# Counting edge pairs: turnings and the logarithm of a pair placed among the next pair's chunks

## The chip, the cores and the metric

The kernel runs on one core of one Trainium2 chip. The metric is the device time of one execution in microseconds (us). Before the change three runs gave 9569.98, 9573.84 and 9581.71 us, so the median is 9573.84 us.

## The reference, cut to what matters

Four graph layers follow each other on 3125 nodes. Three of them read the same edges (103125 with the self loops). The change touches only a preparation whose two results the second and the third layer use.

```python
# layer 1, attention over all edges into a node
e = leaky_relu(alpha_s[src] + alpha_d[dst])
alpha = exp(e - emax[dst]) / (segment_sum(exp(e - emax[dst]), dst)[dst] + eps)
out = segment_sum(xs[src] * alpha, dst)
# layer 2, convolution
agg = segment_sum(h[src], dst)
```

An edge enters either sum as often as it occurs. So both can be written over a dense matrix C, where C[i, j] is the number of edges from j to i: the convolution multiplies by C, the attention adds ln C to its logits. The kernel computes C and ln(C + 2^-60), in which it presses the entries of zero counts far down, and stores both to HBM in f32 as `c.counts` and `c.logs`.

## The kernel before, in words

`count_pairs` (L1078) does this, once, after the edges have been grouped and before the layers. The nodes are ranked into NB = 25 blocks of 128. Two blocks form a pair, so there are PAIRS = 13 of them (the last has one block). The lists of a pair's nodes come in groups of 64 neighbour slots; `steps` (L1136) loads from the tile `groups` how many groups a pair has (`many`) and which is its first (`first`). Every engine runs its own program over the pairs, with semaphores between them.

For each group:

- SP (L1143) loads the ids when DVE has released the one buffer (`ids_free`).
- DVE (L1323) splits an id into high and low part (to L1345), PE transposes the two parts (`split_ps`, L1202), DVE casts them (L1350) and makes `hi_hot` (L1352), a one-hot of the block.
- Then come CHUNKS_OF = 8 chunks of 16 nodes. For each, DVE makes `lo_hot` (`hot`, L1356), PE multiplies the two one-hots in 32 small matmuls (L1212), and ACT copies the sums from PSUM to `counts` (L1243; in a group after a pair's first one DVE adds instead, L1370). `lo_hot` and `chunk_ps` have two buffers each: `hot` of chunk u waits for chunk u - 2 (`counted`), and the matmuls of chunk u wait for the copy of chunk u - 2 (`kept`).

When the chunks of a pair are done, four things follow:

- The turning: PE transposes each block of counts (L1193) in quads of 4 transpositions into one of two PSUM tiles, ACT copies each quad out (L1254). TURNS = 7 quads for each of the two blocks make 14 quads, of 50 transpositions. A quad waits for the copy of the quad two before (`moved`).
- The store of the turned counts, 3.2 MB, issued by ACT (L1258).
- The logarithm, one ACTIVATE by ACT over 6400 elements per partition (L1262).
- `tell`: DVE presses down the zero entries (L1378), then ACT issues the store of the logarithms, 3.2 MB (L1267).

The order is written out by hand in the loops at the end of each engine's program. Quoted from PE and ACT:

```python
with pe.Fori(0, PAIRS // 2 - 1) as two:
    for k in range(2):
        pair(two * 2 + (k + 1))
        turn_counts(two * 2 + k, k, 2)
with act.Fori(0, PAIRS // 2 - 1) as two:
    for k in range(2):
        pair(two * 2 + (k + 2), k)
        finish(two * 2 + (k + 1), 1 - k, two + k)
        tell(two * 2 + k, k)
```

So PE turns pair p after all chunks of pair p + 1, and ACT copies the turned counts and takes the logarithm of pair p there too. DVE runs `pair(p + 2)`, then `tell(p)`. `counts`, `logs` and `turned_sb` have two buffers each.

## Time and profile before

| | before |
|---|---|
| median of 3 runs | 9573.84 us |
| the profiled execution | 9577.8 us |
| its span | 9575.8 us |
| mean granted clock of TensorE | 0.803 of full |
| the stage of `count_pairs` in the span | 1493 to 1899 us |

The profiled execution is 4 us above the median, and 2 us of it lie outside its span. The stage of `count_pairs` is about 4% of the span. The engines in it repeat one pattern from pair to pair, so that it is read from the timeline of one pair, and the stages before and after it are the same program in both kernels.

### The profile page before, as it was taken

What the parts mean: (1) busy time and instruction counts of PE and PEld (TensorE: products, weight loads), DVE (VectorE), ACT (ScalarE), POOL (GpSimd) and SP (SyncE); (2) the same over time, 40 slices, a digit from 0 to 9 for tenths busy, and PEclk for the clock granted to TensorE, in tenths of its full rate; (3) what the DMA queues carried; (4) which work ended last, traced back from release to release, by engine and by line L of the source; (5) the groups of instructions that cost most, each with busy time, mean ns of one, the idle gap of its engine ahead of it and who ended that gap; (6) DMA issues with size and microseconds to landing.
All of it is one profiled execution on the core that took longest, in us unless ns stands there. A gap on an engine that the chain in (4) does not pass through costs nothing. (4 is left out here: it accounts for less than half of the span.)

```text
span 9575.8 us, 217005 instructions
## 1 busy us (share of the span) xinstructions
PE 6368.2 (67%) x63738; PEld 5150.9 (54%) x63739; DVE 7308.4 (76%) x20527; ACT 5592.6 (58%) x12073; POOL 6322.6 (66%) x5522
## 2 busy tenths in 40 slices
PE   3894796555555565546655478878878869467775
PEld 2893796444444444434444355555555544366665
DVE  9779777667777577766777799989989970388886
ACT  4224325546665566656666489979979950144443
POOL 0777773067776777767777578858858850377776
PEclk8555555678887788877788799999999989788887
DMA  0210114622222222222222222212212237232322
GB/s 12 65 53 2 59 61 139 232 48 52 53 52 42 52 52 52 52 43 51 52 52 52 48 56 56 56 50 56 57 42 62 56 93 280 76 53 54 54 54 50
DMA packets 411419, 617.79 MB, mean 65 GB/s; under 512 B 267559, under 2 KB 324353, under 8 KB 387609
## 3 DMA queue, kind: packets, MB, share of 16 engines
q0 software_dynamic: 185232, 370.99, 16.7%
q1 hardware_dynamic: 158592, 160.26, 5.4%
q10 hardware_dynamic: 67497, 85.32, 2.5%
q8 instruction: 50, 0.82, 0.0%
q14 instruction: 48, 0.39, 0.0%
HBM read 513.10 MB, written 104.66 MB: 65 GB/s over the span
## 5 line engine op out<-in xcount | busy, mean ns | idle before, releaser
L914 POOL DMA_INDIRECT l_land<-table,l_words x3504 | 3377.2, 964 | 1115.1 <-issue 1066.6
L1871 POOL DMA_INDIRECT ell<-gat_stage_pay,gat_stage_at x816 | 1657.0, 2031 | 261.8 <-issue 248.4
L1506 PE MATMUL left_product_ps<-k_w,messageT 128*128 128x128 f32 x5136 | 882.4, 324 | 670.8 <-ACT messageT L1541 670.8
L1506 PEld LDWEIGHTS left_product_ps<-k_w,messageT 128*128 128x128 f32 x5136 | 740.9, 222 | 850.3 <-ACT messageT L1541 850.3
L1966 ACT COPY gat_probT<-gat_ps 128x512 f32<-128x512 f32 (+1 forms) x2100 | 1017.2, 552 | 71.6 <-PE gat_ps L1911 62.8
L245 POOL DMA_INDIRECT ell<-pay,position x816 | 843.1, 1033 | 289.3 <-issue 280.0
L1557 ACT ACTIVATE weighed<-kept,l_prob 128x128 f32 x3120 | 988.2, 390 | 68.6 <-ACT l_prob L1059 68.6
L1059 ACT ACTIVATE l_prob<-l_shifted,l_fall 128x9 f32<-128x9 f32 x506 | 153.3, 303 | 1493.5 <-DVE l_fall L1053 1485.5
L2429 PE MATMUL rel_ps<-relation_parts,hot 128*128 128x128 bf16 x11328 | 789.2, 241 | 338.7 <-DVE hot L2530 338.3
L2429 PEld LDWEIGHTS rel_ps<-relation_parts,hot 128*128 128x128 bf16 x11328 | 766.5, 110 | 361.6 <-DVE hot L2530 361.5
L296 PE MATMUL looked_ps<-count,loT_wide 128*128 (+1 forms) x3264 | 755.6, 384 | 47.5 <-issue 44.3
L296 PEld LDWEIGHTS looked_ps<-count,loT_wide 128*128 128x128 f32 x3264 | 744.6, 333 | 56.4 <-issue 53.8
L1911 PE MATMUL gat_ps<-ident,gat_logit 128*128 128x128 f32 x3750 | 579.0, 286 | 254.0 <-ACT gat_logit L1958 242.9
L1669 DVE TENSOR_REDUCE part<-weighed 128x128 f32<-128x1024 f32 x390 | 742.9, 1905 | 0.0
L1917 PE MATMUL gat_ps<-gat_probT,h 128*32 128x128 f32 x15000 | 703.1, 281 | 0.3
L1046 DVE CUSTOM_DVE_ANT_0 product<-right,left_now 128x128 f32<-128x128 f32 x3120 | 697.7, 287 | 0.1
L1911 PE MATMUL gat_ps<-ident,work 128*128 128x128 f32 x3750 | 573.8, 284 | 178.2 <-ACT work L1958 162.5
L354 ACT CAST loT_wide<-loT 128x512 f32<-128x512 bf16 x408 | 252.3, 619 | 700.4 <-PE looked_ps L300 672.4
L1492 PE MATMUL rel_ps<-relation_parts,hotT 128*128 128x256 bf16 x3888 | 659.7, 317 | 2.0 <-ACT hotT L1536 2.0
L1911 PEld LDWEIGHTS gat_ps<-ident,gat_logit 128*128 128x128 f32 x3750 | 408.2, 142 | 419.6 <-ACT gat_logit L1958 275.3
L1500 PE MATMUL left_turned_ps<-ident,message 128*128 128x128 f32 x2568 | 489.8, 323 | 170.3 <-DVE message L1661 170.0
L1911 PEld LDWEIGHTS gat_ps<-ident,work 128*128 128x128 f32 x3750 | 402.8, 140 | 343.2 <-ACT work L1958 247.4
(351 smaller groups left out, 14927.2 us busy)
## 6 DMA issues: line engine op xcount, KB each, us to landing
gcn_edges<-counts SPq DMA_DIRECT2D x50, 1600.0 KB, 8.0
l_land<-table,l_words POOLq DMA_INDIRECT x3504
rows<-low_dram SPq DMA_DIRECT2D x34, 1536.0 KB
counts<-pair_turned_sb ACTq DMA_DIRECT2D x12, 3200.0 KB
logs<-pair_logs ACTq DMA_DIRECT2D x12, 3200.0 KB, 18.2
ell<-pay,position POOLq DMA_INDIRECT x816
ell<-gat_stage_pay,gat_stage_at POOLq DMA_INDIRECT x816
l_words<-ell SPq DMA_DIRECT2D x446, 8.0 KB
```

Of the source, the lines that this page charges most:

```text
L245: pool.indirect_dma_start(c.ells[0][:, :], bass.IndirectOffsetOnAxis(ap=position[:, 0, t:t + 1], axis=0), pay[:, t, :], None).then_inc(pla ...
L296: pe.matmul(looked_ps[r % HALVES][:, j, :], loT_wide[:, r % CAST, j, :], count[:, bass.ds(tile + j, 1), :].rearrange("p a n -> p (a n)"), ...
L914: pool.indirect_dma_start(self.land[:, p, s, :], None, table[:, :], bass.IndirectOffsetOnAxis(ap=self.words[:, p, s, 0:1], axis=0)).then_i ...
L1046: return self.nc.vector.tensor_tensor_reduce(product, rows, own, op0=ALU.mult, op1=ALU.add, scale=-1.0, scalar=0.0, accum_out=self.fall[:, ...
L1506: mm = pe.matmul(right_ps[:, k * H + j, :], messageT[:, k, j, :], k_w[:, :], start=True, stop=True)
L1557: last = nc.scalar.activation(weighed[:, s, :], kept[:, bass.ds(n % 2, 1), s, :].rearrange("p a d -> p (a d)"), ACT.Copy, scale=soft.prob[ ...
L1669: V.tensor_reduce(part[:, :], weighed[:, :, :].rearrange("p s f -> p f s"), AX.X, ALU.add)
L1871: pool.indirect_dma_start(c.ells[1][:, :], bass.IndirectOffsetOnAxis(ap=stage_at[n % 2][:, t:t + 1], axis=0), stage_pay[n % 2][:, t, :], N ...
L1911: mm = pe.transpose(ps[:, q % 4, r * P:(r + 1) * P], logit[t % 2][:, j * P:(j + 1) * P], c.ident[:, :])
L1917: mm = pe.matmul(ps[C * r:C * (r + 1), 4 + t % 2, 0:P], xs[:, 4 * q + r, t * C:(t + 1) * C], probT[:, q % 4 * 4 + r, :], start=(q == 0), s ...
L1966: nc.scalar.copy(probT[:, q % 4 * 4:q % 4 * 4 + rows_of(q), :].rearrange("p r d -> p (r d)"), ps[:, q % 4, 0:rows_of(q) * P]).then_inc(mov ...
L2429: mm = pe.matmul(rel_ps[:, k * H + s, :], hot[:, k, g, s, :], parts[:, g, t, :], start=(g == 0 and t == 0), stop=(g == PARTS - 1 and t == 2))
```

## The change

- `groups` is one word for each pair, `many` in its low and `first` in its high half. `steps` loads one word where it loaded two, on each of four engines, and PE calls it once for each pair instead of twice. DVE packs the word in two more instructions, once.
- PE: `turn_quad` does one quad. In `pair(p)`, after chunks 1, 3, 5 and 7, an `If` for the first group encloses 3, 4, 3 and 4 quads of pair p - 1. Only the 7 quads of the last pair stand alone.
- ACT: in `pair(p)`, the copies of those quads follow the copies of the same chunks. The logarithm of pair p - 1 is in four pieces, after the copies of chunks 2, 4, 6 and 7 (1536, 1536, 1536 and 1792 elements per partition). Before the first piece ACT waits for the store of the logarithms that the buffer held. After the loop it issues the store of the counts.
- DVE: `tell(p - 2)` is in two pieces inside `pair(p)`, before `hot` of chunk 2 and of chunk 5. It counts `told` after the last `hot`, with a drain ahead.
- SP: loads the ids of three pairs, then in turn those of pair p + 3 and, having waited for `told`, stores the logarithms of pair p.

```diff
-        groups = sb("pair_groups", [P, 2, PAIRS], I32)
+        groups, firsts = sb("pair_groups", [P, PAIRS], I32), sb("pair_firsts", [P, PAIRS], I32)
...
+        TELL_AT = {2: slice(0, NB // 2), 5: slice(NB // 2, NB)}
+
+        def quads_of(u):
+            return range(2 * TURNS * (u // 2) // (CHUNKS_OF // 2), 2 * TURNS * (u // 2 + 1) // (CHUNKS_OF // 2)) if u % 2 else ()
+
+        LOG_AT = {u: slice(NB * n // 4, NB * (n + 1) // 4) for n, u in enumerate((2, 4, 6, 7))}
...
-            many = eng.value_load(groups[0:1, 0, bass.ds(p, 1)], min_val=1, max_val=z.bodies)
-            first = eng.value_load(groups[0:1, 1, bass.ds(p, 1)], min_val=0, max_val=z.bodies)
-            return many, first
+            word = eng.value_load(groups[0:1, bass.ds(p, 1)], min_val=1, max_val=(1 << 31) - 1)
+            many = (word & ((1 << HALF_BITS) - 1)).with_bounds(min_val=1, max_val=z.bodies)
+            return eng.snap(many), eng.snap((word >> HALF_BITS).with_bounds(min_val=0, max_val=z.bodies))
...
+                def tell(p, k, parts=2):
+                    sp.wait_ge(told, p + 1)
+                    sp.dma_start(c.logs.rearrange("(h p) j -> p h j", p=P)[:, :, bass.ds(p * (2 * P), parts * P)],
+                                 logs[k][:, :, 0:parts, :]).then_inc(logs_out[k], 16)
+
+                for p in range(3):
+                    pair(p)
+                with sp.Fori(0, PAIRS // 2 - 1) as two:
+                    for k in range(2):
+                        pair(two * 2 + (k + 3))
+                        tell(two * 2 + k, k)
+                tell(PAIRS - 3, 0)
+                tell(PAIRS - 2, 1)
+                tell(PAIRS - 1, 0, 1)
...
-                def turn_counts(p, k, parts):
...
+                def turn_quad(p, k, q):
+                    b, t = q // TURNS, q % TURNS
+                    pe.wait_ge(moved, p * (2 * TURNS) + (q + 1))
+                    for r in range(4 * t, min(4 * t + 4, NB)):
+                        mm = pe.transpose(turned_ps[q % 2][:, r - 4 * t, :], counts[k][:, r, b, :], c.ident[:, :])
+                    mm.then_inc(turned, 1)
+
+                def chunk(n, u):
+                    pe.wait_ge(hot_ready, n * CHUNKS_OF + (u + 1))
+
+                    pe.wait_ge(kept, n * CHUNKS_OF + (u + 1))
...
+                    mm.then_inc(counted, 1)
+
+                def pair(p, k, earlier=True):
                     many, first = steps(pe, p)
                     with pe.Fori(0, many) as g:
                         n = pe.snap(first + g)
...
                         for u in range(CHUNKS_OF):
+                            chunk(n, u)
+                            if earlier and quads_of(u):
+                                with pe.If(g < 1):
+                                    for q in quads_of(u):
+                                        turn_quad(p + (-1), 1 - k, q)
+
+                pair(0, 0, earlier=False)
+                with pe.Fori(0, PAIRS // 2) as two:
                     for k in range(2):
+                        pair(two * 2 + (k + 1), 1 - k)
+                many, first = steps(pe, PAIRS - 1)
+                pe.wait_ge(kept, (first + many) * CHUNKS_OF + 2)
+                for q in range(TURNS):
+                    turn_quad(PAIRS - 1, 0, q)
...
+                def turn_out(p, k, q):
+                    b, t = q // TURNS, q % TURNS
+                    rows = min(4, NB - 4 * t)
+                    act.wait_ge(turned, p * (2 * TURNS) + (q + 1))
+                    nc.scalar.copy(turned_sb[k][:, b, 4 * t * P:(4 * t + rows) * P],
+                                   turned_ps[q % 2][:, 0:rows, :].rearrange("p r d -> p (r d)")).then_inc(moved, 1)
+
+                def send(p, k, parts=2):
+                    act.wait_ge(moved, p * (2 * TURNS) + (parts * TURNS + 2))
+                    act.dma_start(c.counts[bass.ds(p * (2 * P), parts * P), :].rearrange("(b p) i -> p b i", p=P),
+                                  turned_sb[k][:, 0:parts, :]).then_inc(counts_out[k], 16)
+
+                def log(k, rows, parts=2):
+                    return nc.scalar.activation(logs[k][:, rows, 0:parts, :], counts[k][:, rows, 0:parts, :], ACT.Ln,
+                                                bias=few[:, 0:1])
+
+                def pair(p, k, sent=None, again=True):
                     many, first = steps(act, p)
-                    if not unused:
+                    if again and sent is not None:
                         act.wait_ge(logged, p + (-1))
+                    if sent is not None:
+                        act.wait_ge(counts_out[1 - k], sent * 16 + 16)
                     with act.Fori(0, many) as g:
                         n = act.snap(first + g)
                         with act.If(g < 1):
...
+                                if sent is not None:
+                                    for q in quads_of(u):
+                                        turn_out(p + (-1), 1 - k, q)
+                                    if u == min(LOG_AT):
+                                        act.wait_ge(logs_out[1 - k], sent * 16 + 16)
+                                    if u in LOG_AT:
+                                        last = log(1 - k, LOG_AT[u])
+                            if sent is not None:
+                                last.then_inc(logged, 1)
+                    if sent is not None:
+                        send(p + (-1), 1 - k)
+
+                pair(0, 0)
+                pair(1, 1, 0, again=False)
                 with act.Fori(0, PAIRS // 2 - 1) as two:
                     for k in range(2):
+                        pair(two * 2 + (k + 2), k, two + k)
+                pair(PAIRS - 1, 0, PAIRS // 2 - 1)
+                act.wait_ge(counts_out[0], PAIRS // 2 * 16 + 16)
+                for q in range(TURNS):
+                    turn_out(PAIRS - 1, 0, q)
+                send(PAIRS - 1, 0, 1)
...
-                V.tensor_copy(groups[:, 0, :], groups_f[:, :])
-                v.drain()
-                V.tensor_tensor(groups[:, 1, :], ends_f[:, :], groups_f[:, :], ALU.subtract)
+                v.drain()
+                V.tensor_tensor(firsts[:, :], ends_f[:, :], groups_f[:, :], ALU.subtract)
+                v.drain()
+                V.tensor_scalar(firsts[:, :], firsts[:, :], HALF_BITS, None, ALU.logical_shift_left)
+                v.drain()
+                V.tensor_tensor(groups[:, :], firsts[:, :], plan_j[:, :], ALU.bitwise_or)
...
+                def tell(p, k, rows):
+                    v.wait_ge(logged, p + 1)
+                    flat = logs[k][:, rows, :, :].rearrange("p h b j -> p (h b j)")
+                    return V.scalar_tensor_tensor(out=flat, in0=flat, scalar=-NEG, in1=flat, op0=ALU.mult, op1=ALU.min)
+
+                def pair(p, k, earlier=False):
...
                             for u in range(2, CHUNKS_OF):
+                                if earlier and u in TELL_AT:
+                                    tell(p + (-2), k, TELL_AT[u])
                                 v.wait_ge(counted, n * CHUNKS_OF + (u - 1))
                                 hot(u)
+                            if earlier:
+                                v.drain()
+                                v.sem_inc(told, 1)
...
                 pair(0, 0)
                 pair(1, 1)
                 with v.Fori(0, PAIRS // 2 - 1) as two:
                     for k in range(2):
+                        pair(two * 2 + (k + 2), k, True)
+                pair(PAIRS - 1, 0, True)
+                for p in range(PAIRS - 2, PAIRS):
+                    tell(p, p % 2, slice(0, NB)).then_inc(told, 1)
```

On ACT, in the loop over pairs, the compiled program of before has behind the last quads (`pair_turned_sb` is the turned copy, `pair_turned_ps` its PSUM tile):

```order
L1253 REGISTER_ALU
L1254 COPY pair_turned_sb<-pair_turned_ps 128x128
L1257 REGISTER_ALU
L1258 ISA
L1258 DMA counts<-pair_turned_sb 128x2x3200
L1262 ACTIVATE pair_logs<-pair_counts,pair_few 128x6400
L1267 ISA
L1267 DMA logs<-pair_logs 128x25x256
```

The changed one has at the start of a pair and up to the fourth chunk:

```order
L1275 COMPARE_AND_BRANCH
L1277 ISA
L1278 ACT_TABLE_LOAD
L1278 COPY pair_counts<-pair_chunk_ps 128x2x25x16
...
L1255 COPY pair_turned_sb<-pair_turned_ps 128x512
L1277 REGISTER_ALU
L1278 COPY pair_counts<-pair_chunk_ps 128x2x25x16
L1264 ACT_TABLE_LOAD
L1264 ACTIVATE pair_logs<-pair_counts,pair_few 128x1536
L1277 REGISTER_ALU
L1278 COPY pair_counts<-pair_chunk_ps 128x2x25x16
```

The logarithm has moved between the copies of two chunks, and the loop now holds two table loads for each pair; before, the only one of this stage stands ahead of the loop.

On PE, between the last chunk and the first quad, before:

```order
L1212 MATMUL pair_chunk_ps<-pair_hi_hot,pair_lo_hot 128x25 x32
L1198 REGISTER_ALU
L1198 COMPARE_AND_BRANCH
L1137 ISA
L1137 TENSOR_LOAD pair_groups
L1137 ISA x2
L1138 ISA
L1138 TENSOR_LOAD pair_groups
L1138 ISA x2
L1187 ISA
L1191 ISA
L1193 MATMUL pair_turned_ps<-ident,pair_counts 128x128 x4
```

Now, behind the second chunk:

```order
L1215 MATMUL pair_chunk_ps<-pair_hi_hot,pair_lo_hot 128x25 x32
L1231 COMPARE_AND_BRANCH
L1203 ISA
L1205 MATMUL pair_turned_ps<-ident,pair_counts 128x128 x4
L1203 REGISTER_ALU
L1205 MATMUL pair_turned_ps<-ident,pair_counts 128x128 x4
L1203 REGISTER_ALU
L1205 MATMUL pair_turned_ps<-ident,pair_counts 128x128 x4
L1231 UNCONDITIONAL_BRANCH
L1209 REGISTER_ALU
L1215 MATMUL pair_chunk_ps<-pair_hi_hot,pair_lo_hot 128x25 x32
```

The two loads ahead of the quads are gone; a branch stands there, and the next chunks wait behind the quads in PE's order.

## Rows read from the trace of the kernel before

**Rows 1.** The page: span, section 1.

```profile
span 9575.8 us, 217005 instructions
```

**Rows 2.** Waits, stage of `count_pairs`: engine, line, releaser, total us, times, longest.

```profile
DVE pair_splitT L1350 <- PE pair_split_ps L1202: 80.9, 13, 11.5
ACT pair_counts L1243 <- PE pair_chunk_ps L1212: 78.4, 94, 27.1
...
PE pair_chunk_ps L1212 <- DVE pair_lo_hot L1356: 54.9, 51, 3.6
...
ACT pair_logs L1262 <- DMA logs<-pair_logs: 7.7, 1, 7.7
```

**Rows 3.** Timeline of PE: start, us, line and operation, idle before.

```profile
1504.08 0.69 PE L1202 MATMUL pair_split_ps<-ident,pair_split 128*128 128x128 f32 x2 [18.35 <-DVEq L1346]
...
1520.45 0.69 PE L1202 MATMUL pair_split_ps<-ident,pair_split 128*128 128x128 f32 x2 [2.12 <-DVEq L1346]
...
1576.33 0.68 PE L1202 MATMUL pair_split_ps<-ident,pair_split 128*128 128x128 f32 x2 [1.77 <-issue]
1580.57 2.34 PE L1212 MATMUL pair_chunk_ps<-pair_hi_hot,pair_lo_hot 64*128 64x25 bf16 x64 [3.55 <-DVE pair_lo_hot L1356]
...
1588.19 2.36 PE L1212 MATMUL pair_chunk_ps<-pair_hi_hot,pair_lo_hot 64*128 64x25 bf16 x64 [0.18 <-DVE pair_lo_hot L1356]
1592.98 5.24 PE L1193 MATMUL pair_turned_ps<-ident,pair_counts 128*128 128x128 f32 x25 [2.43 <-issue]
1598.69 1.09 PE L1193 MATMUL pair_turned_ps<-ident,pair_counts 128*128 128x128 f32 x8 [0.46 <-ACT pair_turned_sb L1254]
...
1604.41 0.43 PE L1202 MATMUL pair_split_ps<-ident,pair_split 128*128 128x128 f32 x2 [1.40 <-issue]
...
1831.13 0.43 PE L1202 MATMUL pair_split_ps<-ident,pair_split 128*128 128x128 f32 x2 [1.18 <-issue]
```

**Rows 4.** Timeline of DVE: the same columns.

```profile
1589.19 6.82 DVE L1378 SCALAR_TENSOR_TENSOR pair_logs<-pair_logs 128x6400 f32<-128x6400 f32 x1
...
1604.88 0.43 DVE L1350 CAST pair_splitT<-pair_split_ps 128x256 bf16<-128x256 f32 x1 [6.39 <-PE pair_split_ps L1202]
...
1881.29 6.83 DVE L1378 SCALAR_TENSOR_TENSOR pair_logs<-pair_logs 128x6400 f32<-128x6400 f32 x1 [8.85 <-ACT pair_logs L1262]
```

**Rows 5.** Timeline of ACT and of its queue (ACTq).

```profile
1594.98 0.59 ACT L1254 COPY pair_turned_sb<-pair_turned_ps 128x512 f32<-128x512 f32 x1 [0.27 <-PE pair_turned_ps L1193]
...
1603.92 5.64 ACT L1262 ACTIVATE pair_logs<-pair_counts,pair_few 128x6400 f32<-128x6400 f32 x1 [0.61 <-ACT pair_turned_sb L1254]
...
1609.88 1.73 ACT L1243 COPY pair_counts<-pair_chunk_ps 128x800 f32<-128x800 f32 x2 [0.31 <-PE pair_chunk_ps L1212]
...
1878.30 2.96 ACT L1262 ACTIVATE pair_logs<-pair_counts,pair_few 128x3200 f32<-128x3200 f32 x1 [7.73 <-DMA logs<-pair_logs]
```

**Rows 6.** Windows: stretch, us, busy (x count) of PE, PEld, DVE, ACT, POOL, clock, DMA share, GB/s.

```profile
1576.30:1604.40 28.10, 18.91 (x308) 15.85 (x308) 20.38 (x24) 19.06 (x24) 8.21 (x7) 0.64 0.79 266
1592.90:1596.00 3.10, 3.02 (x14) 2.67 (x15) 3.10 (x3) 1.25 (x3) 0.00 (x0) 0.50 1.05 334
1596.00:1599.00 3.00, 2.40 (x16) 1.63 (x15) 2.03 (x14) 2.39 (x5) 0.00 (x0) 0.92 0.22 63
1612.00:1618.00 6.00, 5.58 (x158) 5.36 (x158) 5.59 (x6) 3.96 (x5) 0.00 (x0) 0.50 0.99 333
```

**Rows 7.** Groups by line, in the stage: busy, mean ns, idle before.

```profile
L1352 DVE TENSOR_TENSOR pair_hi_hot<-pair_hi_iota,pair_splitT 128x3200 bf16<-128x3200 bf16 x13 | 23.7, 1826 | 1.0
...
L1262 ACT ACT_TABLE_LOAD x1 | 1.3, 1283 | 0.5 <-ACT pair_turned_sb L1254 0.5
```

**Rows 8.** DMA of the stage: issues with median us to landing; SP's first issue behind it.

```profile
logs<-pair_logs ACTq DMA_DIRECT2D x12, 3200.0 KB, 18.2
...
1899.49 0.87 SPq L2717 DMA_DIRECT2D x<-table_h  x1
```

More of the change, by code:

```diff
@@ L1145, in _, with pair @@
                 sp.wait_ge(plan_ready, 1)
-                def pair(p, _):
+                def pair(p):
                     many, first = steps(sp, p)
@@ L1159, in pair @@
                                          .rearrange("(n p s) c -> p n (s c)", p=P, s=S)).then_inc(ids_in, 16)
-                each_pair(sp, pair)
+                def tell(p, k, parts=2):
[11 more added lines that the diff above has]
+                tell(PAIRS - 1, 0, 1)
+                for k in range(2):
+                    sp.wait_ge(logs_out[k], (PAIRS + 1 - k) // 2 * 16 + 16)
             @block.gpsimd
@@ L1183, in _ @@
                 pe.wait_ge(plan_ready, 1)
-                def turn_counts(p, k, parts):
-                    many, first = steps(pe, p)
-                    pe.wait_ge(kept, (first + many) * CHUNKS_OF + 2)
-                    for b in range(parts):
-                        for t in range(TURNS):
-                            q = b * TURNS + t
-                            pe.wait_ge(moved, p * (2 * TURNS) + (q + 1))
-                            for r in range(4 * t, min(4 * t + 4, NB)):
-                                mm = pe.transpose(turned_ps[q % 2][:, r - 4 * t, :], counts[k][:, r, b, :], c.ident[:, :])
-                            mm.then_inc(turned, 1)
-                def pair(p):
+                def turn_quad(p, k, q):
[7 more added lines that the diff above has]
+                    pe.wait_ge(kept, n * CHUNKS_OF + (u + 1))
+                    for j in range(CHUNK):
+                        for b in range(2):
+                            half = slice(b * GROUP, (b + 1) * GROUP)
+                            mm = pe.matmul(chunk_ps[u % 2][:, b, j * NB:(j + 1) * NB], lo_hot[half, u % 2, :, j],
+                                           hi_hot[half, :, u * CHUNK + j], start=True, stop=True)
+                    mm.then_inc(counted, 1)
+                def pair(p, k, earlier=True):
                     many, first = steps(pe, p)
@@ L1273, in _ @@
+                            if sent is not None:
[4 more added lines that the diff above has]
+                pair(1, 1, 0, again=False)
                 with act.Fori(0, PAIRS // 2 - 1) as two:
                     for k in range(2):
-                        pair(two * 2 + (k + 2), k)
-                        finish(two * 2 + (k + 1), 1 - k, two + k)
-                        tell(two * 2 + k, k)
@@ L1278, in _ @@
-                pair(PAIRS - 1, 0)
-                finish(PAIRS - 2, 1, PAIRS // 2 - 1)
-                tell(PAIRS - 3, 0)
-                finish(PAIRS - 1, 0, PAIRS // 2, 1)
-                tell(PAIRS - 2, 1)
-                tell(PAIRS - 1, 0, 1)
+                        pair(two * 2 + (k + 2), k, two + k)
[3 more added lines that the diff above has]
+                    turn_out(PAIRS - 1, 0, q)
@@ L1373, in pair @@
                                     hot(u + 2)
-                def tell(p, k):
-                    v.wait_ge(logged, p + 1)
-                    flat = logs[k][:, :, :, :].rearrange("p h b j -> p (h b j)")
-                    V.scalar_tensor_tensor(out=flat, in0=flat, scalar=-NEG, in1=flat, op0=ALU.mult,
-                                           op1=ALU.min).then_inc(told, 1)
                 pair(0, 0)
@@ L1384, in _ @@
                     for k in range(2):
-                        pair(two * 2 + (k + 2), k)
-                        tell(two * 2 + k, k)
-                pair(PAIRS - 1, 0)
-                for p in range(PAIRS - 3, PAIRS):
-                    tell(p, p % 2)
+                        pair(two * 2 + (k + 2), k, True)
+                pair(PAIRS - 1, 0, True)
+                for p in range(PAIRS - 2, PAIRS):
+                    tell(p, p % 2, slice(0, NB)).then_inc(told, 1)
 def attention_over_relations(nc, top, z, c, a, x, h, res, work):
```

50 lines of the change are left out of this document (2 added, 48 removed).

## The prediction

> **What bounds the kernel now.** I read the page first: the span is 9575.8 us [rows 1]; the profiled execution took 9577.8 us, 4 us above the median of 9573.84. The stage changed lies between 1493 and 1899 us, so everything here is decided in some 400 us. The waits of that stage come next [rows 2]. Nobody waits for one engine alone: DVE waits 80.9 us for PE's split transpositions, ACT 78.4 us for chunks, PE 54.9 us for DVE's one-hots. So no engine is the bound; a chain that goes from engine to engine is. The timeline of PE shows it for one pair [rows 3]. From the split transpositions at 1576.33 to the first chunk at 1580.57 pass 4.24 us, in which DVE casts and makes hi_hot (1.83 us [rows 7]) and the first lo_hot. The eight chunks run to 1590.55, two in 2.34 to 2.36 us. Then PE idles 2.43 us: end of a loop, two loads of registers, the copy of chunk 7. The 50 transpositions take 1592.98 to about 1603.0, and after 1.40 us more the next split transpositions start, at 1604.41. Sum: 28.1 us a pair. In this cycle DVE is busy 20.4 us and ACT 19.1 us [rows 6].
>
> What hides what: DVE's `tell` of 6.82 us lies beside PE's turning, and DVE still idles 6.39 us behind it before the cast [rows 4]. ACT's logarithm of 5.64 us starts at 1603.92 [rows 5] and lies beside the 4.24 us in which PE and DVE prepare the next pair; chunk copies start 0.31 us behind it. Both are off the chain now.
>
> **The change part by part.** The pieces of `tell` move from hidden to hidden: I cost them at nothing. The first (3072 of 6400 elements, 3.3 us) stands before the third lo_hot, beside the first three quads (2.7 us); the other (3.5 us) lies beside PE's wait below. What they would cost without this cover is up to 6.8 us a pair.
>
> The logarithm is the piece that matters. It leaves the preparation, where ACT has nothing else to do, and goes between copies that PE waits for. From 5.64 us for 6400 elements and 2.96 us for 3200 [rows 5], an ACTIVATE costs 0.28 us plus 0.84 us per 1000 elements; so three pieces of 1536 cost 1.57 us each, the one of 1792 1.78 us. Four pieces are 6.5 us instead of 5.64. The order of the changed program also has a table load before the first copy and before the first piece of every pair. One took 1.28 us [rows 7]. The former lies in ACT's idle preparation and costs nothing while ACT is ahead there by about 1 us; the latter stands between the copies of chunks 2 and 3. The Trainium skill, "ScalarE activation tables: per-element evaluation and per-set limits", section "What a function is on this engine", says that two functions in one set need no switch; the copies between the logarithms of before ran without a load, so the trace agrees. By that rule the loads would be absent and the forecast below would fall by some 12 us; the program's order has them all the same, and I count them.
>
> Now I walk through one pair, time 0 being its split transpositions, with PE at half clock. Chunks: 1.18 us each. Quads: 14 transpositions took 3.02 us at granted clock 0.50 [rows 6], with a hand-over about 0.9 us a quad. Copy of a chunk 0.83 us (two in 1.73 [rows 5]), of a quad 0.59 us plus 0.08.
>
> - Chunks 0 and 1 end at 6.6, quads 0 to 2 at 9.3, chunk 2 at 10.6, chunk 3 at 11.8, quads 3 and 4 at 13.6.
> - ACT: copy of chunk 2 to 11.4, table load to 12.7, piece of the logarithm to 14.3, copy of chunk 3 to 15.1, quad 3 to 15.8. Quad 5 needs the PSUM tile of quad 3, so **PE waits 2.2 us**.
> - Quads 5 and 6 to 16.9, chunks 4 and 5 to 19.4, quads 7 and 8 to 21.2. ACT has copied quad 7 only at 22.1 (a piece lies between chunks 4 and 5): wait 0.9.
> - Quad 9 to 23.0, chunks 6 and 7 to 25.4, quads 10 and 11 to 27.2; quad 10 is copied at 28.1: wait 0.9. Quads 12 and 13 to 29.3.
> - One load of a register instead of two before the next split: 1.40 to 1.77 us in [rows 3]; I take 0.9. That is 30.2. Some ten hand-overs of 0.07 to 0.1 us and the branches of the four `If`s bring it to **31.0 us**.
>
> Against 28.1 us: gone are the 2.43 us before the turning and 0.5 us of loads; back come 4.0 us of waits for ACT, 1.3 us for quads that all run at half clock, and hand-overs. For the `If`s the trace has no row on PE. Bounds: nothing, when PE's sequencer runs ahead, and 2.43 us for a place that holds a branch, two loads and a wait. I take near nothing, since work is queued ahead of each.
>
> Sum over the stage. Pair 0 is as before: 1504.08 to 1520.45 [rows 3]. The eleven cycles to the last pair took 1831.13 - 1520.45 = 310.7 us, and will take 11 x 31.0 = 341.0: **+30.3 us**. The tail: before, from 1831.13 to the end of the last `tell` (1881.29 + 6.83 [rows 4]) 57.0 us and to the next stage's load at 1899.49 [rows 8] 68.4 us, for two pairs' turnings and logarithms stood there, and ACT waited 7.73 us for a store [rows 5]. After: the logarithm of pair 11 ends at 32.5, a table load and 7 quads to 39.6, table load and 2.96 us to 43.9, `tell` to 50.7; the last store of 1.6 MB is a quarter of what takes 18.2 us [rows 8] (counts and logarithms together), 4.6 us, plus 2 for issue and latency: 57.3. **-11.1 us**. Net +19.2 us: 9597.0 for the profiled execution, 9593 for the median.
>
> Packing the word on DVE adds two small operations once, under 1 us. The stores of logarithms now come from SP: issued at about 21 in one cycle, the buffer is needed at 12.7 of the next, 22.7 us later, against 18.2 us [rows 8] with both stores in flight. So no wait. Ids are loaded a pair ahead, with more room.
>
> **The rivals.**
>
> 1. *The clock rises inside the loop.* At 1592.9 the granted clock is 0.50, after 3.1 us of transpositions it is 0.92 [rows 6]; chunks alone leave it at 0.50 [rows 6]. At full clock 8 transpositions take 1.09 us [rows 3], so ACT's copy sets the pace. The waits for ACT stay, and the cycle comes to 30.0 us: 12 us less in all, 9581. Against it: at most four quads stand together, and chunks and waits come between. The Trainium skill, "TensorE: Matmul & The Clock Gate", section "What's actually happening", says that activity releases the throttle, which by itself would bear out this case. Chance 0.22.
> 2. *Faster: PE's waits for ACT vanish.* Place: quads 5, 9 and 12. If ACT's detour between copying chunk 2 and copying quad 3 (4.4 us) were shorter than the 2.2 us that PE needs for chunk 3's end and quads 3 and 4, the cycle would be 27.0 less hand-overs, 26.6 us. That is 11 x (26.6 - 28.24) = -18 us, and the tail is 4.4 shorter: 33.5 us off, 9540. It decides from a cycle of about 27.8 us down. For it: absent table loads together with rival 1; against it: the durations of [rows 5, 7]. Chance 0.13.
> 3. *Branches cost.* At 0.5 us for each `If`, 2 us a pair and 24 us in all: 9617. For it: 1.40 us of [rows 3] are nothing but such work. Against it: the queued matmuls. Chance 0.12.
> 4. *Stores collide.* If logarithms need over 22.7 us to land, ACT waits before the first piece; 2 us a pair give the same 9617. Chance 0.04.
>
> That the change does nothing is excluded: the 13 makings of hi_hot [rows 7] mean one group a pair, so every `If` is taken.
>
> **How the numbers follow.** A measurement of this kernel can tell about 0.2%, 19.1 us. The forecast has 0.49 and stands at that bound; errors of 0.5 us a cycle put it at 9587 to 9599, half on either side, a little more above, for what I left at nothing can only add. Slower: 0.30 of it, and rivals 3 and 4, 0.46. Within 0.2%: 0.19, and 0.22 of rival 1, 0.41. Faster: 0.13. The range goes from 9562, between rivals 1 and 2, to 9614, most of rival 3.
>
> **What would show it.** In the profile after: split transpositions 31 us apart; PE idle before quads 5, 9 and 12 released by the turned copy; 24 table loads or so in the stage; granted clock near 0.5; DVE's `tell` in two forms with no one waiting for it; last `tell` some 50 us behind the last split. Wrong, if the cycle is under 28.1 us, or if the idle time of PE is released by DVE or called issue.

## The result and the profile after

Over seven runs of each, on one chip, the median went from 9577.62 us (9569.98 to 9581.73) to 9613.95 us (9597.9 to 9617.91): ratio 1.0034, 95% interval 1.0025 to 1.0044. So the change makes this kernel slower by 0.34%, 36.3 us. The prediction had 9593.0 us, in a range from 9562.0 to 9614.0, whose upper end the median meets to within 0.05 us, and gave "slower by over 0.2%" 0.46.

The execution that was profiled was the fastest of the seven, 9597.9 us against 9577.8 us before: 20.1 us more, where the forecast had 19.2. The page gives its span, beside which [rows 1] stand:

```profile
span 9596.1 us, 216930 instructions
```

I cut the traces at the first operations of the stages. The stage of `count_pairs` takes 433.0 us instead of 414.9, the three behind it 3542.5, 2378.4 and 435.9 instead of 3540.3, 2376.9 and 437.2, and the rest is the same within 0.2 us. So 18.1 of the 20.3 us of span are where the diff is. The other 16 us between this execution and the median are in no trace. The profiled execution has a mean granted clock of 0.798, the six others have 0.793 to 0.795; whether that goes with the 16 us is not shown.

One pair of the changed kernel, from its split transpositions to the next; the timeline of PE, with the columns of [rows 3]:

```profile
1580.60 0.68 PE L1225 MATMUL pair_split_ps<-ident,pair_split 128*128 128x128 f32 x2 [1.58 <-issue]
1584.83 2.35 PE L1215 MATMUL pair_chunk_ps<-pair_hi_hot,pair_lo_hot 64*128 64x25 bf16 x64 [3.55 <-DVE pair_lo_hot L1384]
1587.11 2.90 PE L1205 MATMUL pair_turned_ps<-ident,pair_counts 128*128 128x128 f32 x12
1590.37 2.35 PE L1215 MATMUL pair_chunk_ps<-pair_hi_hot,pair_lo_hot 64*128 64x25 bf16 x64 [0.36 <-DVE pair_lo_hot L1384]
1592.65 1.97 PE L1205 MATMUL pair_turned_ps<-ident,pair_counts 128*128 128x128 f32 x8
1596.60 1.33 PE L1205 MATMUL pair_turned_ps<-ident,pair_counts 128*128 128x128 f32 x5 [1.98 <-ACT pair_turned_sb L1255]
1597.86 2.22 PE L1215 MATMUL pair_chunk_ps<-pair_hi_hot,pair_lo_hot 64*128 64x25 bf16 x64
1600.01 1.97 PE L1205 MATMUL pair_turned_ps<-ident,pair_counts 128*128 128x128 f32 x8
1602.66 1.12 PE L1205 MATMUL pair_turned_ps<-ident,pair_counts 128*128 128x128 f32 x4 [0.68 <-ACT pair_turned_sb L1255]
1603.71 2.28 PE L1215 MATMUL pair_chunk_ps<-pair_hi_hot,pair_lo_hot 64*128 64x25 bf16 x64
1605.92 1.97 PE L1205 MATMUL pair_turned_ps<-ident,pair_counts 128*128 128x128 f32 x8
1608.54 1.33 PE L1205 MATMUL pair_turned_ps<-ident,pair_counts 128*128 128x128 f32 x5 [0.65 <-ACT pair_turned_sb L1255]
1611.12 0.68 PE L1225 MATMUL pair_split_ps<-ident,pair_split 128*128 128x128 f32 x2 [1.26 <-issue]
```

Chunks and quads alternate as the diff says. PE stops three times for ACT: before quad 5 (1.98 us here, 2.33 to 2.44 in six of ten pairs), before quad 9 (0.68) and before quad 12 (0.65). From the third split, at 1549.75, to the last, at 1856.66, ten cycles take 30.69 us each; before it was 28.33 us. PE also waits 0.36 us for the lo_hot of chunk 2, which DVE makes behind the first piece of `tell`.

Where the first of these stops comes from is to be seen on ACT (the same columns):

```profile
1591.62 0.83 ACT L1278 COPY pair_counts<-pair_chunk_ps 128x800 f32<-128x800 f32 x1 [0.98 <-PE pair_chunk_ps L1215]
1592.47 1.28 ACT L1264 ACT_TABLE_LOAD   x1
1593.77 1.58 ACT L1264 ACTIVATE pair_logs<-pair_counts,pair_few 128x1536 f32<-128x1536 f32 x1
1595.25 0.81 ACT L1278 COPY pair_counts<-pair_chunk_ps 128x800 f32<-128x800 f32 x1
1595.95 1.08 ACT L1255 COPY pair_turned_sb<-pair_turned_ps 128x512 f32<-128x512 f32 x2
```

Between chunk 2's copy and that of quad 3 ACT loads a table and takes a quarter of the logarithm. PE has sent quads 3 and 4 by 1594.6 and stands still until quad 3 is copied.

The waits of the stage, to be read against [rows 2] (engine, line, releaser: total us, times, longest):

```profile
ACT pair_counts L1278 <- PE pair_chunk_ps L1215: 92.8, 68, 27.5
DVE pair_splitT L1378 <- PE pair_split_ps L1225: 67.8, 13, 6.9
PE pair_chunk_ps L1215 <- DVE pair_lo_hot L1384: 51.2, 27, 3.6
PE pair_turned_ps L1205 <- ACT pair_turned_sb L1255: 45.8, 39, 2.6
PE pair_split_ps L1225 <- issue: 14.8, 11, 1.6
```

The fourth row, PE's waits for ACT at the quads, was 17.4 us in the kernel before; the 28 us more are about what the loop has lost. No row of an engine's waits in this stage names a store. The window of the pair above (columns as in [rows 6]), and two rows of the groups of ACT (busy us, mean ns, idle before):

```profile
1580.60:1611.10 30.50, 22.05 (x308) 18.57 (x308) 20.47 (x25) 21.55 (x29) 4.15 (x4) 0.50 0.73 252
```

```profile
L1264 ACT ACT_TABLE_LOAD x13 | 16.7, 1283 | 0.6 <-ACT pair_turned_sb L1255 0.4
L1278 ACT ACT_TABLE_LOAD x12 | 15.4, 1283 | 8.1 <-ACT pair_logs L1264 7.7 <-issue 0.3
```

The granted clock is 0.50, the lower level of 1.2 GHz, over this whole pair; in a pair of the kernel before it was 0.64 [rows 6]. But this is not so in every pair. Another pair, a stretch in it, and the ten cycles together:

```profile
1733.90:1764.90 31.00, 21.61 (x309) 18.23 (x309) 20.50 (x25) 22.40 (x29) 0.00 (x0) 0.56 0.63 221
1744.00:1747.00 3.00, 3.00 (x69) 2.95 (x66) 2.81 (x3) 2.00 (x2) 0.00 (x0) 0.92 0.00 0
1549.75:1856.66 306.91, 217.52 (x3081) 183.63 (x3081) 204.97 (x250) 219.41 (x281) 24.46 (x19) 0.53 0.64 224
```

In six of the ten pairs the clock rises to its upper level for some 3.5 us, here after PE had worked from 1738.18 to 1743.30 (chunks 0 and 1, quads 0 to 2), and the mean of the pair is 0.56. These are the pairs in which PE waits 2.33 to 2.44 us before quad 5. In both kinds of pair chunk 2 starts 9.8 us and quad 5 16.0 us behind the split transpositions: DVE's lo_hot and then ACT set these times, and what PE gains by the clock it spends waiting.

ACT's 21.55 us of work in the first pair holds two table loads; with one more behind the loop, before the copies of the last pair's quads (1888.48), there are 26 in the stage.

The end of the stage, in the timelines of DVE and of SP's queue, to be read against [rows 4, 8]:

```profile
1899.34 6.82 DVE L1349 SCALAR_TENSOR_TENSOR pair_logs<-pair_logs 128x6400 f32<-128x6400 f32 x1 [4.31 <-ACT pair_logs L1264]
```

```profile
1917.74 0.85 SPq L2742 DMA_DIRECT2D x<-table_h  x1
```

and the last store in the list of issues (KB each, us to landing):

```profile
logs<-pair_logs SPq DMA_DIRECT2D x1, 1600.0 KB, 9.7
```

From the last split to the next stage's load pass 61.1 us; before it was 68.4. What lies behind the end of the last `tell` is as long as before: 11.6 us (from 1906.16 to 1917.74) against 11.4 (from 1888.12 to 1899.49 [rows 4, 8]). The queue that carries the stores, in the kernel before from 1888 to 1900 and in the changed one from 1906 to 1918 (packets, MB, share):

```profile
q10 hardware_dynamic: 4362, 2.80, 74.2%
q1 hardware_dynamic: 4367, 2.80, 74.4%
```

In both, 2.80 MB are moved there, some 1.2 MB more than the last store has: the rest of the stores before it is still on its way.

### The profile page after: what moved, and what is told of

The parts are those of the page before. It is cut to its first block and busy times, and to the rows that moved or that the text cites. A ratio compares the mean times of both kernels' runs of the same rounds, so it can differ in the third digit from the quotient of the medians.

```text
span 9596.1 us, 216930 instructions
## 1 busy us (share of the span) xinstructions
PE 6409.2 (67%) x63738; PEld 5190.3 (54%) x63739; DVE 7322.0 (76%) x20539; ACT 5625.0 (59%) x12134; POOL 6326.8 (66%) x5522
## 6 DMA issues: line engine op xcount, KB each, us to landing
logs<-pair_logs SPq DMA_DIRECT2D x12, 3200.0 KB, 11.2
```

## The experiments

The theory: the cycle is a chain through PE, ACT and PE; what it gained by removing PE's 2.43 us before the turning it lost by putting ACT's logarithm and a table load among the copies that PE waits for. The rivals: it is the interleaving itself, at half clock, or the branches, that cost; and, for the 16 us outside the trace, that the changed loop has a slower way of running which the profiled execution did not take.

**A word on the chips.** The runs below were made on three other chips, one group on each. On these the same kernel before takes 12875.66, 12655.4 and 12910.38 us instead of 9577.62. So whole times are given as ratios to the kernel before on the same chip, and a second measure decides: the time from the third split transpositions to the next stage's load `x<-table_h`, read from each trace. The kernel before has 351.7 us there on the first chip, 350.1 and 350.9 on two of the others; the changed one 368.0, and 367.9 and 368.5. So this stretch agrees within 1.6 us where the whole differs by over 3000.

**The changed kernel once more**, unedited.

> The changed kernel once more, for a second trace: of its seven runs one took 9597.9 us (the profiled one) and six 9609 to 9618. Theory A (the stage of the pair counting alone differs between the two kernels): split transpositions 30.5 us apart in this trace too, the stage of count_pairs 18 us longer than before, and whatever is above 9598 lies in other stages, at a lower granted clock of TensorE. Rival (the loop itself has a slower way of running): the split transpositions are 32 us apart in a trace of 9612 us, and no other stage differs.

Measured: 12856.33 us, ratio 0.999 [0.9977, 1.0003]. The cycle is 30.68 us, as on the first chip, 367.9 us by the second measure. So the loop has no slower way that shows here; that rival has nothing for it. The clock in its ten cycles is 0.51 in the mean where it was 0.53 in the first trace, with the same cycle. The ratio is another than on the first chip though the loop costs the same: something outside the loop weighs as much as the change.

**No table loads in the loop.** One logarithm of one column ahead of the loop; the compiler then puts one load into the stage instead of 26.

```diff
-        few = sb("pair_few", [P, 1])
+        few, first_ln = sb("pair_few", [P, 1]), sb("pair_first_ln", [P, 1])
...
+                nc.scalar.activation(first_ln[:, :], few[:, :], ACT.Ln, bias=few[:, 0:1])
```

> One Ln of a single column stands ahead of ACT's loop, so that the compiler places no table load inside it (the program has 1 for this stage instead of 10, 24 of them executed). Theory A (the load between the copies of chunks 2 and 3 is on the chain): PE's wait for ACT before quad 5 falls from 2.0-2.4 us to about 0.8, the cycle from 30.5 to 29.3 us, the tail loses 2.6 us: 15 to 17 us less than the changed kernel. Rival (loads lie in idle time of ACT): the cycle stays at 30.5 us and at most the 2.6 us of the tail are won.

Measured: ratio 0.9993 [0.9982, 1.0005]; cycle 29.30 us; 352.65 us, 15.3 less than the changed kernel. Quad 5 now starts 14.6 us behind the split transpositions instead of 16.0. In the pair shown PE waits 0.58 us before it; in most pairs in which the clock rises it is 1.38 to 1.45, for 2.33 to 2.44 before:

```profile
2664.90 0.68 PE L1225 MATMUL pair_split_ps<-ident,pair_split 128*128 128x128 f32 x2 [1.60 <-issue]
...
2679.50 1.33 PE L1205 MATMUL pair_turned_ps<-ident,pair_counts 128*128 128x128 f32 x5 [0.58 <-ACT pair_turned_sb L1256]
```

A table load between copies costs 1.4 us a pair, its full 1.28 us and a little more. As all of the gain lies before quad 5 and one load explains it but for 0.1 us, the one in the preparation cost next to nothing, as forecast. The tail lost 1.5 us, where 2.6 were expected.

**The logarithm whole, behind chunk 7**, without table loads and with them. It then stands beside the next pair's preparation again, as in the kernel before, while the quads stay among the chunks.

```diff
-        LOG_AT = {u: slice(NB * n // 4, NB * (n + 1) // 4) for n, u in enumerate((2, 4, 6, 7))}
+        LOG_AT = {7: slice(0, NB)}
```

> As ln_first, and the logarithm of pair p-1 is one ACTIVATE behind all copies of pair p, where it lies beside the preparation of the next pair, as before the change; the quads stay among the chunks. Theory A (what costs is the logarithm between the copies, not the quads among the chunks): PE waits for ACT before quads 5, 9 and 12 fall from 3.3 us in all to under 0.5, cycle 27.2 us or less, 33 to 40 us under the changed kernel and 0 to 10 us under the kernel before in the loop and 11 to 15 us in the tail. Rival B (interleaving itself costs: PE's strict order, quads at half clock): the cycle stays above 29 us.

Measured: ratio 0.9971 [0.9956, 0.9987]; cycle 27.41 us; 333.5 us. That is 34.5 us less than the changed kernel on the same chip and some 17 less than the kernel before on the others. The cycle is 0.2 us above what was expected, and the tail 9.0 us shorter than that of the kernel before, not 11 to 15.

```profile
2690.06 0.68 PE L1225 MATMUL pair_split_ps<-ident,pair_split 128*128 128x128 f32 x2 [1.20 <-issue]
...
2714.70 1.22 PE L1205 MATMUL pair_turned_ps<-ident,pair_counts 128*128 128x128 f32 x5 [0.38 <-ACT pair_turned_sb L1256]
...
2717.63 0.68 PE L1225 MATMUL pair_split_ps<-ident,pair_split 128*128 128x128 f32 x2 [1.70 <-issue]
```

```profile
2689.32 5.66 ACT L1265 ACTIVATE pair_logs<-pair_counts,pair_few 128x6400 f32<-128x6400 f32 x1
2695.56 0.83 ACT L1279 COPY pair_counts<-pair_chunk_ps 128x800 f32<-128x800 f32 x1 [0.58 <-PE pair_chunk_ps L1215]
```

The whole logarithm is done 0.58 us before ACT gets the first chunk of the next pair, so PE does not wait for it.

**The same with the table loads.**

> As log_last_ln_first but with the compiler's table loads in the loop: two for each pair, one before the logarithm and one before the first copy of the next pair. Theory A: both now lie in a row with the logarithm (1.28 + 5.64 + 1.28 us plus 0.9 us between), 9.1 us beside a preparation of 5.5 us up to the first copy, so that copy is 1.5 to 2.5 us late: cycle 28.5 to 29.5 us, 12 to 22 us under the changed kernel. Rival (loads cost nothing anywhere): the same cycle as log_last_ln_first.

Measured: ratio 0.9989 [0.9977, 1.0001]; cycle 28.74 us; 350.4 us. In ACT's timeline the load at L1278 now does delay the first copy:

```profile
2662.09 1.28 ACT L1264 ACT_TABLE_LOAD   x1
2663.38 5.66 ACT L1264 ACTIVATE pair_logs<-pair_counts,pair_few 128x6400 f32<-128x6400 f32 x1
2669.53 1.28 ACT L1278 ACT_TABLE_LOAD   x1 [0.49 <-ACT pair_logs L1264]
2670.82 1.55 ACT L1278 COPY pair_counts<-pair_chunk_ps 128x800 f32<-128x800 f32 x2
```

The four kernels on this chip make a square, in us a pair:

| logarithm | with table loads | without |
|---|---|---|
| four pieces among the copies | 30.68 | 29.30 |
| whole, behind chunk 7 | 28.74 | 27.41 |

The place of the logarithm costs 1.9 us in both columns, the loads 1.3 to 1.4 in both rows. With the quads among the chunks and the logarithm in its old place the cycle is 27.41 against 28.2 us before, so the rival that expected over 29 us from the interleaving falls. The 27.41 are not the interleaving alone: this kernel also has the packed word, which an experiment below finds to be worth 1.2 us a pair in the changed kernel. The interleaving by itself may then be no gain at all; it was not run by itself.

**The kernel before, the changed kernel and the best of the square together**, on another chip, with a new one beside them.

> The kernel before, unchanged, for its trace on the chip of this call. Theory A: split transpositions 28.2 us apart in the steady loop, on any chip (the changed kernel has 30.7). What the whole execution takes can differ from chip to chip (9577 us on one, 12876 us on the next for the same kernel); by theory A the added time lies outside the steady loop of the pair counting, in waits called issue. Rival: on a chip where the whole is slow the loop of before is slower too, above 29 us, which would explain why there the changed kernel was not slower than before (ratio 0.999).

Measured: ratio 1.0001 [0.9989, 1.0013]; cycle 28.17 us; 350.1 us.

> The changed kernel, unchanged, beside before_again on the same chip. Theory A: loop 30.7 us; from the third split transpositions to the next stage's load 368 us against 351.7 us of before; the first two pairs depend on the chip (46 us on the first, 77 us on the second). Rival: some other stage differs by over 5 us between the two traces of this call; then that stage, and not the loop, holds the rest of the 36 us by which the medians of the first measurement differ.

Measured: ratio 1.0086 [1.0068, 1.0104], 115 us by the medians, far more than on the first chip; cycle 30.72 us, 368.5 us: 18.4 more than the kernel before, as on the first chip. Yet the stage of `count_pairs` is longer by 28.8 us, the other 10 in its first two passes, and the attention over relations, where the diff changes nothing, by 98 us (5033.2 against 4935.1). On this chip the rival holds: another stage differs, and by far more than the loop.

> The kernel of log_last_ln_first once more (logarithm whole behind all copies, one Ln ahead of the loop), beside before_again. Loop 27.4 us, 333 to 334 us from the third split to the next load: 18 us under before and 34.5 us under the changed kernel on any chip; ratio to before 0.998 on a fast chip.

Measured: ratio 1.0076 [1.0051, 1.0101]; cycle 27.31 us; 332.8 us, and a stage 8.4 us shorter than before. Here the attention over relations takes 5028.5 us, 93 more, which hides that gain; the expected ratio was 0.998. On these chips, then, a ratio alone would mislead.

**Two quads ahead of the first chunk.** PE still idles some 3.5 us behind the split transpositions. This edit, on top of the last, turns quads 0 and 1 of the pair before in that gap, twelve others among the chunks, three at a time, and cuts `tell` in three.

```diff
-        TELL_AT = {2: slice(0, NB // 2), 5: slice(NB // 2, NB)}
+        TELL_AT = {2: slice(0, NB // 3), 4: slice(NB // 3, 2 * NB // 3), 6: slice(2 * NB // 3, NB)}
+        AHEAD = 2
...
                         mm.then_inc(split_turned, 1)
+                        if earlier:
+                            with pe.If(g < 1):
+                                pe.wait_ge(kept, n * CHUNKS_OF + 2)
+                                for q in range(AHEAD):
+                                    turn_quad(p + (-1), 1 - k, q)
...
                         with act.If(g < 1):
+                            if sent is not None:
+                                for q in range(AHEAD):
+                                    turn_out(p + (-1), 1 - k, q)
```

> As best_1, and quads 0 and 1 of the earlier pair stand between the split transpositions and chunk 0, where PE idles 3.5 us, the other 12 quads three by three; tell in three pieces. Theory A (PE's own work and the 3.5 us idle of the preparation are the chain now): two quads of 0.9 us each leave the chain and so does most of the 0.8 us wait for the lo_hot behind the second piece of tell: loop 25.0 to 25.8 us, 20 to 28 us under best_1. Rival B (ACT becomes late: 5.65 us of logarithm, then two copies of quads before the copy of chunk 0): gain under 0.8 us a pair, and PE waits for ACT before chunk 2. Rival C: DVE becomes the chain (20.5 us busy in 27): PE idles before chunks on lo_hot, loop 26 us.

Measured: 12625.13 us, ratio 0.9976 [0.9964, 0.9989]; cycle 25.20 us; 313.9 us, 36.2 less than the kernel before. One pair on PE:

```profile
2611.68 0.68 PE L1227 MATMUL pair_split_ps<-ident,pair_split 128*128 128x128 f32 x2 [2.10 <-issue]
2612.16 1.91 PE L1207 MATMUL pair_turned_ps<-ident,pair_counts 128*128 128x128 f32 x8
2615.92 2.35 PE L1217 MATMUL pair_chunk_ps<-pair_hi_hot,pair_lo_hot 64*128 64x25 bf16 x64 [1.85 <-DVE pair_lo_hot L1395]
...
2637.07 0.68 PE L1227 MATMUL pair_split_ps<-ident,pair_split 128*128 128x128 f32 x2 [1.54 <-issue]
```

and the window of this pair, with the columns of [rows 6]:

```profile
2611.68:2637.07 25.39, 21.54 (x309) 18.59 (x309) 20.36 (x26) 18.72 (x24) 0.00 (x0) 0.50 0.77 267
```

PE is busy 21.54 of 25.39 us at half clock in this pair; the pairs beside it have 0.63 and 0.57 and take 25.16 and 25.01 us. The 25.2 us are 3 us under the kernel before. How much of the 2.1 us under best_1 is due to the two quads and how much to the third piece of `tell` was not separated.

> The kernel of head_quads again, for its ratio beside before_third and the runs of before on this chip: loop 25.2 us, from the third split to the next load 314 us, 36 us under before in the stage; ratio 0.996 to 0.998 where the other stages stay as they are.

Measured, on a third chip: 12854.89 us, ratio 0.9957 [0.9941, 0.9974], a little more gain than expected; cycle 25.21 us; 314.0 us, 36.9 less than the kernel before beside it. It has the lowest median of the study on both chips where it ran, though on this one the interval overlaps with that of the kernel with two words below. On the first chip it was not run.

**Next to no work added.** The kernel before, with 40 increments of a semaphore added once at the start of the stage on each of SP, PE, ACT and DVE: 160 small instructions, which no loop repeats.

```diff
+                for _ in range(40):
+                    pe.sem_inc(turns, 1)
```

> The kernel before with 40 increments of a semaphore that nobody waits for at the start of the pair counting on SP, PE, ACT and DVE: the same work, the code behind it lies elsewhere. Theory C (where the code lies changes the waits called issue in the long loop of the attention over relations): the loop of the pair counting stays at 28.2 us a pair, the attention over relations (on two slow chips 4935 to 5100 us, depending on the kernel) differs by over 20 us from that of before_third in this call, or on a fast chip by 5 to 20 us. Rival (the changed stage itself, its data or its timing, disturbs the later stage): all stages within 5 us of before_third.

Measured: ratio 1.0141 [1.0126, 1.0155]; cycle 28.07 us.

> The kernel before, unchanged: what a second trace on a third chip differs by. Loop 28.2 us, from the third split to the next load 350 to 352 us. Beside the runs of before of the same call it says how far two identical kernels lie apart: ratio 1.000 within 0.15%.

Measured: ratio 1.0012 [0.9999, 1.0025]; cycle 28.23 us; 350.9 us. The attention over relations in the first and in the second of these two (columns as in [rows 6]):

```profile
2947.00:8185.00 5238.00, 2309.66 (x13113) 1877.14 (x13113) 2558.07 (x11073) 2254.94 (x5786) 2538.36 (x2643) 0.68 0.15 34
```

```profile
2918.40:8019.00 5100.60, 2496.29 (x13113) 2028.34 (x13113) 2567.42 (x11073) 2268.75 (x5786) 2546.40 (x2643) 0.66 0.15 35
```

The same instructions in the same numbers, no engine busy for longer, and 137 us more. The loop of `count_pairs` stays as it is; the stage as a whole takes 21 us more (467.0 against 446.3): DVE waits 43.2 us for its first ids instead of 2.7, and part of that is made up in the next two cycles. The 40 increments hold DVE itself for 3.7 us. The added increments can act on a later stage by where its code lies or by when it starts; no run separates the two, so that it is the place of the code is only argued. But on this chip an edit that adds next to no work costs 1.4%, four times what this change cost on the first.

**Two words again**, in the changed kernel.

```diff
-            word = eng.value_load(groups[0:1, bass.ds(p, 1)], min_val=1, max_val=(1 << 31) - 1)
...
+            many = eng.value_load(groups[0:1, 0, bass.ds(p, 1)], min_val=1, max_val=z.bodies)
+            first = eng.value_load(groups[0:1, 1, bass.ds(p, 1)], min_val=0, max_val=z.bodies)
...
```

> The changed kernel without the packed word (steps loads two registers as before). Theory A (the loads between the last quad and the next split transpositions lie on PE's chain): PE's idle time there rises from 1.2-1.65 us by 0.3 to 0.6, loop 31.0 to 31.3 us against 30.7, 4 to 7 us in all. Rival (the sequencer's time there is the ends of loop and branch, not the load): the same 30.7 us.

Measured: ratio 0.9968 [0.9956, 0.998]; cycle 31.93 us; 380.6 us. Two splits of its timeline, to be compared with the 1.26 and 1.58 us above:

```profile
2663.18 0.68 PE L1225 MATMUL pair_split_ps<-ident,pair_split 128*128 128x128 f32 x2 [2.80 <-issue]
...
2695.04 0.69 PE L1225 MATMUL pair_split_ps<-ident,pair_split 128*128 128x128 f32 x2 [2.55 <-issue]
```

The expectation was too low: in this kernel the second load costs 1.2 us a pair, 12 to 13 us in the stage. It is no fixed price: the kernel before has two loads in this place too, and only 1.40 and 1.77 us of idle time [rows 3]. The prediction had credited the packed word with 0.5 us a pair against the kernel before; measured from there, 1.26 and 1.58 us are 0.15 to 0.2 less. Why two loads cost so much more behind the `If` is open. (The ratio is below one though the stretch is 30 us longer than before: the attention over relations took 95 us less than in the run beside it.)

## Why the prediction was right, and where it was off

- *A chain from engine to engine is the bound, and the logarithm moved onto it.* Right, and shown: with the logarithm alone put back beside the preparation the cycle falls by 1.9 us, without the table loads by 1.4, and with both the stretch from the third split to the next load is 17 us shorter than that of the kernel before instead of 16 to 18 longer.
- *The cycle: 31.0 us.* 30.69, from about 30.5 and 30.9 in turn. The wait before quad 5 was put at 2.2 and is 1.98 to 2.44; quad 5 was put at 15.8 us behind the split and starts at 16.0. Those before quads 9 and 12 were put at 0.9 each and are 0.65 to 0.68: too large by 0.5 us together. The load before the next split was put at 0.9 and is 1.17 to 1.65, with the branches' cost in it, too small by 0.5. Two errors of one size and opposite signs: that the sum came out better than its terms is luck.
- *The loop: +30.3 us over eleven cycles.* 1856.66 - 1520.26 = 336.4 instead of 310.7: +25.7. Of the 4.6 us between them, 3.1 are ten cycles 0.31 us under 31.0, and 1.5 the first cycle, still 29.49 us, where I took the steady one for all eleven.
- *The tail: 57.3 us.* To the end of the last `tell` it was 49.5, against 50.7 forecast; but the next stage's load comes 11.6 us behind that, not 6.6. The mis-sized term is the last store. I took 4.6 us, a quarter of a median for four times the bytes, plus 2 for which no row was given; issue to landing took 9.7, and 1.9 us more passed to the load. The store does not travel alone: 2.80 MB were still to be moved, not its 1.6. The rows had the answer, for the kernel before has the same last store and needed 11.4 us in this place. So the tail saved 7.3 us, not 11.1. Here too, two errors, of 4.6 and 3.8 us, cancel by luck: 18.1 us for the stage, 19.2 forecast.
- *The clock: half, in the whole loop.* Not so. It rose in six of ten pairs (0.56 in such a pair, 0.53 over the ten cycles), though at most four quads stand together and chunks come between, which had been the argument against rival 1. What falls is the rival's price, 1 us a pair: quad 5 starts 16.0 us behind the split with and without the rise, because PE waits for DVE's lo_hot and for ACT. The other trace of the same kernel has 0.51 and the same cycle, with 30.5 and 30.9 us in turn there too. The forecast of the time was right here for another reason than the one given. The rule of the Trainium skill, "TensorE: Matmul & The Clock Gate", section "What's actually happening", that activity releases the throttle, is borne out in those six pairs and says nothing of the time, which other engines set.
- *Table loads.* 26, where "24 or so" stood. The rule of the Trainium skill, "ScalarE activation tables: per-element evaluation and per-set limits", section "What a function is on this engine", that two functions in one set need no switch, was rightly not counted on: the loads are in the program and each takes its 1283 ns. The trace agrees with the rule in one respect, for with one logarithm ahead of the loop the copies and logarithms ran on without any.
- *`tell` hidden before and after.* Nearly. Its pieces took 3.35 us at 1585.83 and 3.62 us at 1592.77, where 3.3 and 3.5 had been put. The second is hidden, beside PE's wait before quad 5. Behind the first, PE waits 0.36 us for the lo_hot of chunk 2, a wait that the sum left at nothing.
- *No wait for stores.* Right: median 11.2 us to landing, against the 22.7 us there were; rival 4 falls. Rival 3, 0.5 us a branch, has no room either: PE does not idle before quads 0, 3, 7 and 10, which stand right behind the branches, and all that stands before a split, the load among it, is 1.2 to 1.65 us.
- *The median.* The trace accounts for 20 of 36 us. The median stands at the very edge of the range, which reached so far only for rivals 3 and 4, and neither of them came: that it lies within is luck. The loop itself was the same in every trace of four chips. That an edit with next to no work of its own can cost later stages more than this is shown on another chip; that something of the kind is in the 16 us on the first is only argued, for its profiled execution does not have them. It stays open.

## What to carry to other kernels

Before moving work off a crowded place, look at what it stood beside: a long operation that ran while its engine had nothing else to do is free there, and cut into four it is paid for at each place where another engine waits. Where the last store of a stage stays as it was, its time is read from the kernel before and not worked out from bytes. A raised clock gave nothing here, where other engines set the time. Table loads in a loop are read from the changed program, not from a rule; here one logarithm of a single column ahead of the loop removed them. Where the whole time depends on the chip, or on an edit that adds next to no work, judge a local change by a stretch of the trace that agrees from chip to chip, and take the whole only beside an unedited twin.

## What was not expected of the hardware

- The same kernel took 9577.62 us on one chip and 12655 to 12910 us on three others, while the cycle of this loop agreed within 0.3 us (28.07 to 28.33, the edited twin among them). Part of the added time is in waits that the profile calls "issue", in stages other than this loop: on the second of these chips `PE left_product_ps` has 161 of them in the attention over relations, 411.6 us in all, 9.2 us the longest, where on the first chip no such group is among the largest. But the waits of the same matmuls for ACT's `messageT` have grown too, from 670.8 to 1414.8 us, and this stage is 1395 us longer. Why the chips differ stays open.
- 160 increments, done once, made the kernel 1.4% slower on the one chip where this was tried.
- The second load of a register, behind a branch, cost 1.2 us on PE, nearly as much as all that stands before a split in the changed kernel.
- In one and the same loop, pairs at a granted clock of 0.50 throughout and pairs with a rise (0.56) follow each other, and quad 5 starts 16.0 us behind the split in both; in the loop with two quads ahead a pair at 0.50 had PE busy 21.54 of 25.39 us.
